# First attention of a language-model block: one exponential per step over both key halves instead of two

## What is computed

```python
AC = jnp.einsum('bhid,bhjd->bhij', Q, K)
BD_full = jnp.einsum('bhid,md->bhim', Q, Er_emb)
BD = BD_full[:, :, i_idx, m_idx]
scores = (AC + BD) / math.sqrt(dk)
attn = jax.nn.softmax(scores, axis=-1)
out = jnp.einsum('bhij,bhjd->bhid', attn, V)
```

## Time and profile before

| | |
|---|---|
| median of 3 runs | 915.25 us (914.11 to 917.23) |
| profiled execution, its own time | 919.9 us |
| its span, first to last instruction | 917.8 us |
| mean granted TensorE clock | 0.935 of full speed |
| TensorE matmul busy | 811.5 us, 88% |
| ScalarE busy | 337.1 us, 37% |
| VectorE busy | 464.6 us, 51% |
| first attention, first to last subtraction | 40.3 to 255.8 us |

### The profile page before, as it was taken

How to read it: one execution, slowest core, us unless ns; L and a number is a source line. 1 busy time by engine, 2 the same in 40 slices (tenths; PEclk the granted TensorE clock), 3 DMA queues, 4 the chain that set the end, 5 groups by cost and what they waited for, 6 DMA issues and landing times. The chain is left out here.

```text
span 917.8 us, 19246 instructions
## 1 busy us (share of the span) xinstructions
PE 811.5 (88%) x7380; PEld 547.7 (60%) x7381; DVE 464.6 (51%) x1079; ACT 337.1 (37%) x568; POOL 148.4 (16%) x155
## 2 busy tenths in 40 slices
PE   4899999999988996999998878875989999999994
PEld 2466666666667874666666764542556666666662
DVE  7666665655536553667664773610124444444441
ACT  5566666666623443455543222200111111111110
POOL 4000000000003341000000220174002222222222
PEclk7599999999979997999998897987999999999997
DMA  5200000000011565699981600023012222222221
GB/s 199 94 2 2 2 2 2 2 2 2 4 41 35 135 129 114 89 181 172 163 176 53 217 1 14 12 107 125 24 34 46 46 46 46 46 46 46 46 40 18
DMA packets 68493, 58.88 MB, mean 64 GB/s; under 512 B 5504, under 2 KB 60104, under 8 KB 68432
## 3 DMA queue, kind: packets, MB, share of 16 engines
q1 hardware_dynamic: 60512, 47.60, 23.1%
q0 software_dynamic: 7152, 9.38, 6.2%
q10 hardware_dynamic: 768, 1.02, 0.4%
HBM read 35.02 MB, written 22.95 MB: 63 GB/s over the span
## 5 line engine op out<-in xcount | busy, mean ns | idle before, releaser
L1124 DVE TENSOR_REDUCE fa_m<-ps 128x2 bf16<-128x512 f32 x128 | 81.7, 684 | 35.1 <-PE ps L1022 34.4
L1365 POOL DMA_INDIRECT out<-ex_Y,ex_to x39 | 60.6, 1554 | 215.9 <-DVE ex_Y L1615 212.8
L1104 ACT ACTIVATE fa_PT<-ps 128x1024 f32<-128x1024 f32 x64 | 65.6, 1024 | 68.2 <-PE ps L1040 68.2
L624 ACT ACTIVATE la_PT<-ps 128x512 f32<-128x512 f32 x128 | 69.5, 594 | 33.4 <-PE ps L530 33.4
L1433 PE MATMUL ps<-WG,ex_xT 128*128 x156 | 74.4, 600 | 0.6 <-ACT ex_xT L1493 0.6
L1446 PE MATMUL ps<-WD,ex_hT 128*128 x312 | 73.9, 380 | 0.9 <-DVE ex_hT L1599 0.9
L1433 PE MATMUL ps<-WU,ex_xT 128*128 x156 | 74.2, 598 | 0.0
L1495 ACT ACTIVATE ex_sl<-ps 128x512 f32<-128x512 f32 x39 | 23.3, 597 | 135.1 <-PE ps L1433 135.1
L657 DVE TENSOR_REDUCE la_m<-ps 128x4 bf16<-128x512 bf16 x64 | 44.3, 692 | 48.6 <-PE ps L523 47.6
L1595 DVE TENSOR_TENSOR ex_hd<-ps,ex_sl 128x512 f32<-128x512 f32 x39 | 27.0, 692 | 80.2 <-PE ps L1433 80.2
L638 DVE CAST V<-ps 96x512 bf16<-96x512 f32 x64 | 44.0, 687 | 38.0 <-PE ps L495 38.0
(11 more groups left out here) (255 smaller groups left out, 1417.1 us busy)
## 6 DMA issues: line engine op xcount, KB each, us to landing
QK<-qk_parts SPq DMA_DIRECT2D x96, 128.0 KB, 5.0
qk_parts<-pj_parts SPq DMA_DIRECT2D x16, 384.0 KB, 2.7
expert_in<-zfill SPq DMA_DIRECT2D x1, 5070.0 KB, 16.1
ex_XR<-expert_in SPq DMA_DIRECT2D x39, 130.0 KB
WG<-in_e_gate SPq DMA_DIRECT2D x8, 512.0 KB, 9.0
WU<-in_e_up SPq DMA_DIRECT2D x8, 512.0 KB, 9.6
WD<-in_e_down SPq DMA_DIRECT2D x8, 512.0 KB, 8.9
out<-HS SPq DMA_DIRECT2D x4, 512.0 KB, 3.1
```

The source lines that it names most:

```text
L624: nc.scalar.activation(PT[:, n % 2, jh], ps[:, 2 * (n % 2) + jh], ACT.Exp, scale=QK_SCALE).then_inc(s_exp[jh], 1)
L1104: nc.scalar.activation(PT[:, grp % 2, k:k + 2], ps[:, 2 + 2 * (hp % 2):4 + 2 * (hp % 2)].rearrange("p k (j i) -> p k j i", j=2), ACT.Exp, ...
L1124: nc.vector.reduce_max(m[:, par, h], ps[:, h % 2].rearrange("p (f j) -> p f j", f=2), AX.X).then_inc(s_max, 1)
L1365: nc.gpsimd.indirect_dma_start(out=outs, out_offset=bass.IndirectOffsetOnAxis(ap=to[:, n:n + 1], axis=0), in_=Y[:, n], in_offset=None, com ...
```

## The change

A step's two exponentials become one over both halves (1024 columns in two neighbouring banks, written to both halves of PT). `s_ready` and `s_exp` become one semaphore each: `s_ready` is raised by the last of the eight subtracting matmuls, and `s_exp` by the single exponential. `build(n, 0)`, both `sum_levels` and the end wait on it; `build(n, 1)` follows `build(n, 0)` on the same engine and has no wait of its own on the exponentials any more.

```diff
-    s_built, s_ready, s_exp = ([sem("la_" + n + k) for k in names(2)] for n in ("built", "ready", "exp"))
+    s_built, s_ready, s_exp = [sem("la_built" + k) for k in names(2)], sem("la_ready"), sem("la_exp")
...
-                    if n >= 2:
-                        pe.wait_ge(s_exp[jh], n - 1)
+                    if n >= 2 and jh == 0:
+                        pe.wait_ge(s_exp, n - 1)
...
                         for q in range(4):
                             last = mm(ps[:, 2 * (n % 2) + jh, q * P:(q + 1) * P], m[:, n % 2, q:q + 1].to_broadcast([P, P]), g.negIB[:],
                                       start=False, stop=True, skip_group_check=True)
-                        last.then_inc(s_ready[jh], 1)
+                    last.then_inc(s_ready, 1)
...
-                    pe.wait_ge(s_exp[jh], n + 1)
+                    pe.wait_ge(s_exp, n + 1)
...
-                        pe.wait_ge(s_exp[0], N)
-                        pe.wait_ge(s_exp[1], N)
+                        pe.wait_ge(s_exp, N)
...
-                    for jh in range(2):
-                        act.wait_ge(s_ready[jh], n + 1)
-                        nc.scalar.activation(PT[:, n % 2, jh], ps[:, 2 * (n % 2) + jh], ACT.Exp, scale=QK_SCALE).then_inc(s_exp[jh], 1)
+                    act.wait_ge(s_ready, n + 1)
+                    nc.scalar.activation(PT[:, n % 2], ps[:, 2 * (n % 2):2 * (n % 2) + 2], ACT.Exp, scale=QK_SCALE).then_inc(s_exp, 1)
```

## The result

The changed kernel takes 934.17 us (median of 4 runs, 933.47 to 935.99) against 915.85 us for the kernel before (median of 4, 914.11 to 917.23). The ratio is 1.0204, with a 95% interval from 1.018 to 1.0228: slower, by 18.3 us. The whole interval lies above 1; whether the change costs more or less than 2% stays open. The forecast was 934.

What follows compares the result with a forecast made beforehand. TensorE, in fixed instruction order, was taken to set the pace, so waits in its queue are paid. The terms 8.8+4.0+2.5+2.0+0.5+1.0 = 18.8 us, added to 915.25, gave 934.0 us; range 925 to 942.

Steps and rivals of the forecast that it cites:

- The merged exponential lasts 1.02 us: Step's exponential on ScalarE: 1024 ns, as in the second attention, against 1.08 to 1.09 us for the pair.
- both bounds of 10 us: Merged exponential's cost: 1188 ns without the pair's overlap, +10 us; 0.86 us without any fixed part, -10 us.
- t+0.66: Exponential's start, counted from the step's first subtracting matmul, t: after all eight subtractions, in place of t+0.43.
- t+1.74: Earliest start of the next build on TensorE, counted from the first subtraction; 1.34 before in plain steps.
- The sum: Delays over all kinds of step, step 0 and the end: 18.8 us in a stage of some 220.
- By kind, in the same order: Plain steps 8.8 us, steps with a weigh 4.0, ahead of chunk starts 2.5, steps 59 to 61 2.0, subtraction 62 0.5.
- After subtraction 63: End of the stage: the last sums wait for the merged exponential, first at t+1.74, second at 2.10: +0.5 us.
- Step 0: First step, at the lower clock: build at 2.13 against 1.67, +0.5 us.
- The slack: Rival: slack in builds outside chunk starts and the end absorbs most of the delay; 6.0 us slower, 921 us; chance 0.05.
- The saved fixed cost: Rival: one exponential saves 0.06 us per step on ScalarE, 3.9 us in all, giving 911 us; chance 0.04.
- The clock stayed at 1.00: Rival: short pauses on TensorE lower its clock to the half level, some 70 us more, near 985; chance 0.02.
- TensorE does its other work in the shadow and has no slack of its own: Each step: TensorE works during the reduction, so whatever delays the build delays the next step by the same amount.

Runs made afterwards that it cites:

- e6: Kernel before, with units made six steps ahead in place of five and TensorE's order unchanged: 904.54 us, ratio 0.989.
- e1: Kernel before, with only `s_ready` made one semaphore, raised by the eighth subtraction; two exponentials and two `s_exp` kept: 919.17 us, ratio 1.0051.
- e4: Changed kernel with TensorE's order altered: turn first, both builds, weigh, subtractions, unit, then both sums of the previous step: 900.18 us, ratio 0.9839.
- e5: Kernel before (two exponentials, signals per half) with TensorE's order altered: turn, both builds, weigh, subtractions, unit, both sums: 899.2 us, ratio 0.9818.
- e3: Changed kernel with its exponential cut back into two of 512 columns, both signals still shared: 937.74 us, ratio 1.024.

## Why the prediction was right

Point by point, against its own steps.

- *The merged exponential lasts 1.02 us.* 1024 ns. The row of the second attention priced it exactly, and both bounds of 10 us were wider than needed. The formula of the Trainium skill (ScalarE: Activation LUTs, "What ACT_TABLE_LOAD costs") gave 1039; the measurement decides.
- *It starts at t+0.66 and the build goes at t+1.74.* Both as forecast, in plain and weigh steps alike, and 1.64 us lie between build and next subtraction as before.
- *The sum.* Steps 1 to 62 were to give 8.8+4.0+2.5+2.0+0.5 = 17.8 us. By kind, in the same order, the two timelines differ by 8.71+3.85+2.45+1.96+0.50 = 17.47. After subtraction 63 I expected 0.5. VectorE's copy, which waits for the last sums, started 2.07 behind it (257.86 - 255.79) and now starts 2.44 behind it (274.96 - 272.52), so 0.37. The two rows, before and after:

```profile
257.86 0.69 DVE L649 COPY HS<-ps 128x512 f32<-128x512 f32 x1 [2.19 <-PE ps L543]
...
274.96 0.69 DVE L647 COPY HS<-ps 128x512 f32<-128x512 f32 x1 [3.07 <-PE ps L543]
```

- *Step 0.* Here the step failed: +0.5 was forecast, and it got 0.76 shorter (4.14 to 3.38), because the clock rose earlier in this execution. Its eight subtractions took 1.03 us in the profile of before and 0.62 in the profile after. The windows of step 0, before, after and in e6, which has the order and the signals of before:

```profile
40.30:44.44 4.14, 4.14 (x49) 3.35 (x47) 2.32 (x4) 2.27 (x4) 0.00 (x0) 0.57 0.01 2
...
40.32:43.70 3.38, 2.69 (x46) 1.94 (x46) 2.02 (x4) 2.10 (x3) 0.00 (x0) 1.00 0.01 2
...
40.80:43.53 2.73, 2.69 (x46) 1.95 (x47) 1.97 (x4) 2.05 (x4) 0.00 (x0) 1.00 0.00 0
```

I take the clock of step 0 for chance of the execution and not the kernel's doing: e1 and e6, in the order of before, ran it at 1.00 too, and e4 and e5, alike but for the exponential and its signals, at 1.00 and 0.61. The mean granted clock also differs between executions of one kernel: 0.938 to 0.958 in the four of the changed one. No two profiles of one kernel are on record, so for step 0 this isn't shown. At equal clock, against e6, the merged kernel's step 0 is 0.65 us longer (3.38 - 2.73), near the forecast +0.5. With the chance of the clock, and 1.0 us less in the stages behind, the profiled execution moved from 919.9 to 935.99, 16.1 us, where 18.8 was forecast and the medians moved 18.3.
- *Luck.* The stage, its end and step 0 at equal clock give 17.47 + 0.37 + 0.65 = 18.5 us, close to the 18.8 of the forecast and the 18.3 of the medians. That 934.0 met 934.17 even more closely is in part luck: the median of the kernel before came out 0.6 us higher than the 915.25 I had added to, and the move 0.5 smaller.
- *The rivals.* The slack was 0.26 and didn't absorb 0.66; e1 shows what it can absorb, a lateness of 0.23. The saved fixed cost is real, 0.06 per step or 3.8 us of the stage (e3), against the 21.25 that the two shared signals cost. The clock stayed at 1.00.
- *What I had not seen:* "TensorE does its other work in the shadow and has no slack of its own" was true of that order alone. Work placed ahead of the build covers the merged exponential, and the work itself isn't fixed at 2.98 us a step: grouped otherwise it takes 2.73 (e4).

## What to carry to other kernels

Merging two instructions of a consumer merges two releases too: price the later start (all inputs ready) and the later end of the first part against the saved fixed cost, here 0.66 us against 0.06. What counts is the slack between that end and the reader's place in its queue, so read it first from one step of each kind, and if the merge is wanted, move work that doesn't depend on it ahead of the reader. A wait that ends late behind another engine's queue (the chunk starts) can be removed by making the input one step earlier: one constant took 11 us off here (e6), and the engine itself needed no change.

## What the runs showed of the hardware

Eight summing matmuls (fp32, 32-column weights) take 0.36 us until the next group starts, and the last matmuls of the group ahead of them are followed 0.31 to 0.33 later in place of 0.21 to 0.24; sixteen in one group take 0.58. It is 0.36 as well where the next group is the weigh, which is also fp32 but has 32x32 weights (151.47 to 151.83 in the kernel before), so it isn't only the change of type. With the order of e4 the plain step was 0.24 us shorter (2.98 to 2.74) at the same instructions. Which part of TensorE takes this time at the change was not tried.

A 1024-column exponential over two PSUM banks took 1024 ns; two of 512 back to back took 1.08 to 1.09 us from start to end.
